# Row means from the rounded input, image row sums taken in the statistics pass, and a new order of TensorE's work in a two-layer convolution kernel

## What is computed

```python
# layer 0
n = 127.0
scale_input = max(abs(x_n)) / 128            # over the whole batch, x_n = group norm of x
x_q = round(clip(x_n / scale_input, -n, n))
acc = conv3x3(x_q, weight_int8)              # zero padding 1
x = x + acc * (scale_input * scale_weight) + bias
# layer 1
X = rfftn(group_norm(x), axes=(-2, -1))      # real and imaginary parts
Yr = conv3x3(Xr, wr) - conv3x3(Xi, wi) + b_real
Yi = conv3x3(Xr, wi) + conv3x3(Xi, wr) + b_imag
x = x + irfftn(Yr + i Yi)
```

## Time and profile before

| | us |
|---|---|
| median of 3 runs | 3694.32 (3689.42 to 3700.12) |
| the profiled execution, its own time | 3688.6 |
| its span in the profile | 3686.8 |
| TensorE busy (matmuls) | 2952.2, 80% of the span |
| VectorE busy | 3147.2, 85% |
| ScalarE busy | 1888.0, 51% |
| POOL busy | 1481.3, 40% |
| DMA | 730.98 MB, mean 198 GB/s |

### The profile page before, as it was taken

The page is one execution under the profiler, slowest core; times in us unless marked ns, Lnnn a source line. Parts: engine busy times, 40 slices in busy tenths (PEclk is TensorE's granted clock), DMA queues, the critical chain, the costliest instruction groups (busy, mean ns, idle before and its releaser), DMA issues.

```text
span 3686.8 us, 126585 instructions
## 1 busy us (share of the span) xinstructions
PE 2952.2 (80%) x45732; PEld 2630.6 (71%) x45732; DVE 3147.2 (85%) x5880; ACT 1888.0 (51%) x2799; POOL 1481.3 (40%) x1984
## 2 busy tenths in 40 slices
PE   0000004899999999999999999999999999999998
PEld 0000002688888888888888888888888888888888
DVE  8999995688888888888888888888888888888886
ACT  8999991344444444444444444444444444444443
POOL 4777100344444444434443333443443433344444
PEclk9999999999999999999999999999999999999999
DMA  8777760366666666666666666666666666666655
GB/s 312 239 239 239 239 216 13 100 205 197 201 199 203 202 200 200 204 197 200 201 202 195 197 194 193 202 197 197 204 199 196 204 194 192 201 193 206 199 181 180
DMA packets 630696, 730.98 MB, mean 198 GB/s; under 512 B 76752, under 2 KB 602160, under 8 KB 614736
## 3 DMA queue, kind: packets, MB, share of 16 engines
q1 hardware_dynamic: 482640, 588.71, 50.1%
q10 hardware_dynamic: 147456, 134.28, 12.7%
HBM read 262.58 MB, written 134.22 MB: 108 GB/s over the span
## 4 chain that ended last, share of the span: by engine, by line
PE 54%; SPq 13%; DMA 11%; issue 11%; DVE 7%; ACTq 1%; ACT 1%; POOL 1%; DVEq 0%; POOLq 0%
PE y_ps L986 14%; PE mean_b L1031 9%; PE x_ps L973 7%; PE conv_ps L1018 7%; SPq L464 7%; PE fin_ps L1005 6%; DMA halo<-quant 4%; DMA out<-img 4%; PE t_ps L964 4%; SPq L386 3%; PE conv_ps L1020 2%; DVE scaled L763 2%; DMA img<-in_x 2%; PE fin_ps L1000 2%; DVE scaled L764 1%
## 5 line engine op out<-in xcount | busy, mean ns | idle before, releaser
L734 POOL TENSOR_SCALAR eo<-img,norm 128x256 f32<-128x256 f32 x512 | 477.9, 933 | 1458.5 <-PE t_ps L964 1248.9
L986 PEld LDWEIGHTS y_ps<-mix_w,stack 128*128 128x128 f16 x24576 | 793.5, 99 | 119.6 <-DMA stack<-xn 6.0
L986 PE MATMUL y_ps<-mix_w,stack 128*128 128x64 f16 x24576 | 809.3, 194 | 4.5 <-DMA stack<-xn 4.4
L562 ACT ACTIVATE y_hi<-y_ps 128x512 f16<-128x512 f32 x512 | 305.6, 597 | 889.3 <-PE y_ps L986 889.3
L548 ACT ACTIVATE xt<-t_ps 128x512 f32<-128x512 f32 x512 | 305.7, 597 | 629.2 <-PE t_ps L964 506.6
L973 PE MATMUL x_ps<-dft,xt 128*128 128x128 f32 x4096 | 541.6, 275 | 0.0
L839 DVE SCALAR_TENSOR_TENSOR img<-conv_ps,cst,img 128x512 f32<-128x512 f32 x512 | 383.1, 748 | 169.3 <-PE conv_ps L1020 153.1
L1031 PE MATMUL mean_b<-row_mean,img 128*128 128x48 f32 x4096 | 512.8, 273 | 8.4 <-DVE img L839 8.4
L1031 PEld LDWEIGHTS mean_b<-row_mean,img 128*128 128x128 f32 x4096 | 504.1, 196 | 18.2 <-DVE img L839 17.5
L826 DVE SCALAR_TENSOR_TENSOR xn<-x_ps,norm,xn 128x512 f16<-128x512 f32 x512 | 383.7, 750 | 140.7 <-ACT xn L555 120.0
L973 PEld LDWEIGHTS x_ps<-dft,xt 128*128 128x128 f32 x4096 | 498.3, 192 | 0.0
(11 more groups left out here) (134 smaller groups left out, 5111.6 us busy)
## 6 DMA issues: line engine op xcount, KB each, us to landing
stack<-xn SPq DMA_DIRECT2D x2048, 132.0 KB, 2.7
img<-in_x SPq DMA_DIRECT2D x1024, 128.0 KB, 2.9
out<-img ACTq DMA_DIRECT2D x1024, 128.0 KB, 3.0
img<-in_x SPq DMA_DIRECT2D x120, 1024.0 KB, 4.9
halo<-quant SPq DMA_DIRECT2D x192, 193.3 KB, 3.3
halo<-quant SPq DMA_DIRECT2D x64, 169.1 KB, 3.2
row_mean<-table_row_mean SPq DMA_DIRECT2D x1, 768.0 KB, 15.4
spread<-table_spread SPq DMA_DIRECT2D x1, 512.0 KB, 14.6
```

The lines of the kernel that those rows point to most:

```text
L734: nc.gpsimd.tensor_scalar(even, rows[:, :, 0:F], norm[v][:, 2:3], None, ALU.add).then_inc(shift_s, 1)
L986: last = nc.tensor.matmul(y_ps[t % 2][:, g, b, :], stack[:, t % 2, g, first:first + F], mix_w[:, 2 * at + b, g, f, part, :], start=i == 0, ...
```

## The change

- The row means no longer come from the image after layer 0. They are put together from two parts. The weighted row sums of x itself are taken in the first phase (`image_means`): TensorE multiplies each image by the wave table as it passes, in fp32 (the table has 48 columns and is the weights, 256 image columns pass), ScalarE copies the 48 x 256 result out of PSUM, and SyncE writes it to DRAM (`keep`). In the second phase SyncE reads it back (`load_means`). The sums of the convolution follow from the same weighted sums of the rounded input: `row_means` multiplies the 16-bit rounded input by a 16-bit table of 128 columns, and `mean_rows` combines them with weights that POOL derives from the weights of layer 0.
- The waits of the first phase are extended: a quarter is reloaded only when TensorE is done with it too.
- ScalarE's scaling writes 16-bit integers (`whole`), which does the rounding; VectorE only limits them. quant and halo are fp16 instead of bf16.
- In TensorE's step, the convolution, its row means and the first group sum stand behind the mix; in VectorE's step `round_pair` stands ahead of `layer0_pair`.

```diff
-MEANS_OF = {14: (0, 1), 15: (2, 3), 0: (4, 5), **{t: (t + 5,) for t in range(1, 11)}}
-TABLES = ("dft", ..., "row_mean", ...)                   # 14 tables
+TABLES = ("sums_runs", "sums", "dft", ..., "coef_a", "rounded_w", ...)   # 17 tables
...
-        quant = sb("quant", [P, HB, HW], bf16)
-        halo = sb("halo", [96, HB, HW], bf16)
+        quant = sb("quant", [P, HB, HW], f16)
+        halo = sb("halo", [P, HB, HW], f16)
+        rounded_w = sb("rounded_w", [P, HB, P], f16)
+        rmx = sb("rmx", [48, 2, N])
...
+        whole = flat(scaled[:]).bitcast(mybir.dt.int16)[:, 0:2 * N].rearrange("p (a w) -> p a w", a=2)
...
         @block.sync
+            sp.dma_start(sums[1], table["sums_runs"]).then_inc(runs_s, 16)
             for u in range(2):
                 for q in range(QU):
                     load_runs(u + 2, u, q)
...
+            for g in range(R):
+                sp.dma_start(raw_a[C * g:C * g + C].rearrange("p o a b -> p o (a b)"), flat0).then_inc(weight_s, 16)
+            sp.dma_start(scale_o, scale_weight[None, :].to_broadcast([P, C])).then_inc(weight_s, 16)
...
+            def keep(n, k, u):
+                sp.wait_ge(sums_s, n + 3)
+                sp.dma_start(kept[k], rmx[:, u, :]).then_inc(kept_s[u], 16)
+
+            def load_means(k, u):
+                if not (isinstance(k, int) and k == 0):
+                    sp.wait_ge(meanc_s, k)
+                sp.dma_start(rmx[:, u, :], kept[k]).then_inc(rmx_s[u], 16)
...
+                        sp.wait_ge(p1_pe, (2 * i + u - 2) * QU + q + 1)
                         load_runs(2 * i + u + 2, u, q)
+                    keep(2 * i + u - 2, 2 * i + u, u)
...
                 for t in range(PAIRS):
+                    if t == 6 and conv:
+                        load_means(s + 1, 1 - u)
...
         @block.scalar
+                act.wait_ge(p1_pe, QU * (n + 1))
+                act.wait_ge(kept_s[u], 16 * (i + 1))
+                nc.scalar.activation(rmx[:, u, :], sums_ps[u], ACT.Copy).then_inc(sums_s, 1)
...
-                act.wait_ge(rounded_s, PAIRS * k + j)
-                nc.scalar.activation(scaled[:], img[u][:, 2 * j:2 * j + 2, :], ACT.Identity,
+                act.wait_ge(quant_s, PAIRS * k + j)
+                nc.scalar.activation(whole, img[u][:, 2 * j:2 * j + 2, :], ACT.Identity,
                                      bias=b0[:, bass.ds(k, 1)], scale=a0[:, bass.ds(k, 1)]).then_inc(scaled_s, 1)
...
+                    if conv and t == STATS_AT - 1:
+                        act.wait_ge(rq_s, PAIRS * (s + 3))
+                        nc.scalar.activation(rq[:], rq_ps, ACT.Identity, scale=q_scale).then_inc(rqe_s, 1)
...
         @block.vector
                 if not first:
-                    dve.wait_ge(conv_s, PAIRS * k + QP * (c + 1))
+                    dve.wait_ge(rq_s, PAIRS * k + QP * (c + 1))
                     dve.wait_ge(halo_s[c], 32 * k)
                 dve.wait_ge(scaled_s, PAIRS * k + j + 1)
                 rows = quant[:, 2 * j:2 * j + 2, 1:N + 1]
-                nc.vector.tensor_scalar(rows, scaled[:], MAGIC, MAGIC, ALU.add, ALU.subtract).then_inc(rounded_s, 1)
-                dve.wait_ge(rounded_s, PAIRS * k + j + 1)
-                nc.vector.tensor_scalar(rows, rows, CLIP, -CLIP, ALU.min, ALU.max).then_inc(quant_s, 1)
+                nc.vector.tensor_scalar(rows, whole, CLIP, -CLIP, ALU.min, ALU.max).then_inc(quant_s, 1)
...
+                    if conv if t < PAIRS - AHEAD else ahead:
+                        d, jq = quant_of(t)
+                        round_pair(s + d, jq, isinstance(i, int) and s + d == 0)
                     d, c = conv_of(t)
                     if conv if d == 1 else ahead:
                         layer0_pair(s + d, (u + d) % 2, c)
                     if conv and t == STATS_AT:
                         stats_var(s + 1)
-                    if conv if t < PAIRS - AHEAD else ahead:
-                        d, jq = quant_of(t)
-                        round_pair(s + d, jq, isinstance(i, int) and s + d == 0)
...
         @block.tensor
+            def image_means(i, u, tab):
+                n = 2 * i + u
+                for q in range(QU):
+                    pe.wait_ge(load_s[u][q], loaded(i))
+                    if q == 0:
+                        pe.wait_ge(sums_s, n + 1)
+                    for hb in range(QB * q, QB * q + QB):
+                        last = nc.tensor.matmul(sums_ps[u], tab[:, 48 * hb:48 * hb + 48], img[u][:, hb, :],
+                                                start=hb == 0, stop=hb == HB - 1)
+                    last.then_inc(p1_pe, 1)
...
-            def row_means(k, u, c):
-                pe.wait_ge(x1_s, done(k, c))
+            def row_means(k, c):
+                pe.wait_ge(quant_s, PAIRS * k + c + 1)
                 if c == 0:
-                    pe.wait_ge(meanc_s, k + 1)
-                    nc.tensor.matmul(mean_b[:, 0:96], ident[:], zeros[:], start=True, stop=False)
+                    pe.wait_ge(rqe_s, k + 1)
                 for hb in (2 * c, 2 * c + 1):
-                    for half in range(2):
-                        nc.tensor.matmul(mean_ps[half], img[u][:, hb, F * half:F * half + F], row_mean[:, hb, :],
-                                         start=False, stop=False)
+                    last = nc.tensor.matmul(rq_ps, rounded_w[:, hb, :], quant[:, hb, :], start=hb == 0, stop=hb == HB - 1)
+                last.then_inc(rq_s, 1)
-            def centre_rows(k, u):
+            def mean_rows(k, i, u):
+                pe.wait_ge(rmx_s[u], 16 * (i + 1))
+                pe.wait_ge(rqe_s, k + 2)
                 pe.wait_ge(zb_s, k + 1)
                 for half in range(2):
+                    for dw in range(3):
+                        nc.tensor.matmul(mean_ps[half], rq[:, F * half + dw:F * half + dw + F], conv_a[:, dw, :],
+                                         start=dw == 0, stop=False)
+                    nc.tensor.matmul(mean_ps[half], rmx[:, u, F * half:F * half + F], ident[0:48, 0:48], start=False, stop=False)
                     last = nc.tensor.matmul(mean_ps[half], norm[u][:, 2:3].to_broadcast([P, P]), channel[:],
...
                     if conv and t == IMAGE_AT:
-                        centre_rows(s + 1, 1 - u)
-                    d, means = means_of(t)
-                    if conv if d == 1 else ahead:
-                        for c in means:
-                            row_means(s + d, (u + d) % 2, c)
+                        mean_rows(s + 1, i + u, 1 - u)
+                    if conv and t == IMAGE_AT + 2:
+                        mix_rows(s + 1)
+                    if runs(mix, conv, t + 1):
+                        mix_pair(s, t + 1)
                     if conv and t == STATS_AT:
                         group_stat(s + 1, meane_s, 0, gmean_s)
                     d, c = conv_of(t)
                     if conv if d == 1 else ahead:
                         conv_pair(s + d, c)
-                    if conv and t == IMAGE_AT + 2:
-                        mix_rows(s + 1)
-                    if runs(mix, conv, t + 1):
-                        mix_pair(s, t + 1)
+                        for m in range(c) if d == 2 and c == 1 else ():
+                            row_means(s + d, m)
+                        if d == 1 or c:
+                            row_means(s + d, c)
```

More of the change, by code:

```diff
@@ L85, in shape_tables @@
             for r in range(R):
-                rm[:, r, b, j, :] = eye * wave[j, R * b + r] / N
-    tab["row_mean"] = rm.reshape(P, HB, 3 * C)
+                rm[0, :, r, b, j, :] = eye * wave[j, R * b + r] / N
+                rm[1, :, r, b, j, :] = eye * wave[j, HB * r + b] / N
+    tab["sums"], tab["sums_runs"] = rm.reshape(2, P, HB * 3 * C)
+    rw = np.zeros((P, HB, P), np.float16)
+    hi, lo = halves(RSCALE * N * rm[0].reshape(P, HB, 3 * C))
+    rw[:, :, 0:48], rw[:, :, 48:96] = hi, lo
+    for c in range(C):
+        rw[R * c, 0, 96 + c] = 1.0
+        rw[R * c + R - 1, HB - 1, 112 + c] = 1.0
+    tab["rounded_w"] = rw
+    ca = np.zeros((8, C, 3, 3))
+    for dh in range(3):
+        co, si = np.cos(th * (dh - 1)), np.sin(th * (dh - 1))
+        turn = np.array([[1, 0, 0], [0, co, si], [0, -si, co]])
+        for part in range(2):
+            ca[3 * part:3 * part + 3, :, :, dh] = (turn.T / (RSCALE * N))[:, None, :]
+    ca[6, :, :, 2] = -wave[:, N - 1] / N
+    ca[7, :, :, 0] = -wave[:, 0] / N
+    tab["coef_a"] = ca.reshape(P, 9)
     tab["channel"] = np.concatenate([np.repeat(eye, R, 0), np.zeros((P, 2 * C))], 1) / (2 * R)
@@ L147, in shape_tables @@
     tab["coef_i"] = ci
[L149 removed]
+    half = ("inv", "spread", "first_row", "rounded_w")
     return {n: np.ascontiguousarray(v, dtype=np.float16 if n in half else np.float32) for n, v in tab.items()}
@@ L169, in build @@
     table = {k: nc.inline_tensor(v, name=f"table_{k}").ap() for k, v in shape_tables().items()}
+    kept = nc.dram_tensor("kept", (samples, 48, N), fp32, kind="Internal").ap()
     ctx = ExitStack()
@@ L242, in build @@
```

(20 more changed lines are left out.)

68 lines of the change are left out of this document (46 added, 22 removed).

## The result

The changed kernel takes **3660.0 us** (median of 6 runs, 3651.4 to 3672.5) against 3693.3 us (3686.2 to 3701.8) for the kernel before, measured in turn on the same chip: ratio 0.991, 95% interval 0.9885 to 0.9935. It is faster, but by 33 us and not by 206; the time is outside the predicted range. The profiled execution after has a span of 3649.5 us, against 3686.8: 37.3 us less.

The account below looks back on a forecast made before the run. The prediction took TensorE to bound the kernel, with SyncE's DMA-issuing queue close below and the bound afterwards. 3688.6 - 194 (steady stage) + 12 (start) - 25 (first image) + 2 (end) = 3483, at the median 3488 us; range 3335 to 3612.

Parts of the forecast that it names:

- SyncE's waits in the sum for the period: Steady stage: SyncE's 86.1 to 89.7 us plus at most some 2 of waits gives 88 a period, 194 us gained in all.
- TensorE's stall at step 10: Steady stage: the variance matmul waits for VectorE's late layer 0, about 2 us a period, for which TensorE has room.
- TensorE's work: Steady stage: row means go and smaller matmuls come, so TensorE's busy time falls from 90.7 to 82.4 us a period.
- VectorE: Steady stage: rounding goes, limit on integers takes 0.30 us; busy time falls from 80.0 to 72.8 us a period, hidden.
- Start: Before the third image: added tables and weight DMAs on SyncE, 10.5 us, and 1.8 MB more to move; +12 us.
- First image: First image's convolution: row means of 1.94 us leave the loop 16 times, less halo waits and longer mean_rows; -25 us.
- End: End of the kernel, from 3593 us on, without convolution: +2 us for mean_rows.
- The two engines hinder each other: Rival, steady stage: SyncE flat out at 89.7 us plus 2 of waits, period 92, median 3612 us; chance 0.18.
- No gain in the steady stage: Rival: SyncE's issues lengthen with the rate and eat everything, 3678 to 3690 us; chance 0.04.
- TensorE stays the bound: Rival, steady stage: SyncE's long issues shrink as stores spread out, period 83.5 us, median 3348 us; chance 0.20.
- SyncE's long issues: Single SyncE issues up to 2203 ns (median 603), taken as waits for ScalarE's stores through a shared descriptor generator; period then nearer 86.1.
- The half-rate first phase: Rival, first phase: TensorE at half rate needs 28.5 us an image instead of 17.6, median 3838 us; chance 0.08.

Follow-up runs that it names:

- a_stats_first: The changed kernel with VectorE's group variance ahead of `layer0_pair` at step 10; 3581.3 us, ratio 0.970 to the kernel before.
- a_half_loads: The changed kernel with one of the two image loads of each step issued by ScalarE instead of SyncE; 3513.6 us, ratio 0.950 to the kernel before.
- b_round: The kernel before with only the rounding done by ScalarE's 16-bit integer write, VectorE keeping just the limit; 3696.5 us, ratio 0.9996.
- b_no_means: The kernel before without the fp32 row means except for the first pair (30 of 32 row blocks left out); 3642.7 us, ratio 0.983.
- a_order_old: The changed kernel with the old order of TensorE (convolution ahead of mix) and VectorE (`layer0_pair` ahead of `round_pair`); 3700.9 us, ratio 1.001 to the kernel before.
- b_order_new: The kernel before with TensorE's row means, convolution and first group sum moved behind the mix; 3826.3 us, ratio 1.035.
- b_order_nomeans: The kernel before with row means, convolution and first group sum behind the mix, and 30 of 32 row blocks left out of the means; 3640.0 us, ratio 0.981.
- a_loads_act: The changed kernel with both image loads of a step issued by ScalarE, behind its stores, instead of SyncE; 3533.2 us, ratio 0.955 to the kernel before.

## Why the prediction was wrong

**The step that failed** is SyncE's waits in the sum for the period: "I take 88 us a period, between 86.1 and 89.7, with no waiting on top of the upper and some 2 us on top of the lower". It measured 93.75. SyncE's work was right (85.2 us; predicted 86.1, with one DMA more than before). The waits were wrong, 8.5 us in place of 2. I had argued that the loads "shed most of that" because the stores come 1.7 us earlier in the step. They shed 1.5 us a period, and waits for the mix gave 1.1 of it back. The mistake in kind was to split 94.3 us into 85.4 of work and 8.9 of slack. This queue, which works in order and needs 85 to 87 us of 94, did not absorb a stall of two microseconds that comes every period. In the changed kernel too it ran eight steps in 43.5 us, 5.44 us each as in the earlier trace rows, right behind a pause of 2.7 us:

```profile
1509.77 2.56 SPq L519 DMA_DIRECT2D stack<-xn  x4
1515.00 1.39 SPq L417 DMA_DIRECT2D img<-in_x  x2
...
1558.53 1.39 SPq L417 DMA_DIRECT2D img<-in_x  x2
```

a_stats_first shows it from the side of the wait, a_half_loads from the side of the work. What the remaining 5.6 us of waits for stores come from (the latency of the landing, or the place of the store in ScalarE's step) no run tells apart.

**TensorE's stall at step 10** was foreseen ("about 2 us a period on TensorE, which now has room for it"), 2.08 us measured. That TensorE had room for it was the second error: the next restacking waits for the mix behind it, so it went through SyncE's queue to everything. And nothing in my sum had the fall of the clock in the steady stage, where all figures were taken at full rate. **TensorE's work** was right: predicted 82.4 us, measured 85.0, of which 98.7 / 2000 x 93.75 / 2 = 2.3 are half rate, leaving 82.7.

**VectorE** 72.1 us (predicted 72.8). The limit on integers takes 0.32 us on average (0.31 in the kernel before), ScalarE's integer write 0.80, as its fp32 write did; b_round confirms that in the total it's worth nothing. **Start** +10.2 (predicted +12): VectorE's second idle time is 14.5 us, was 6.27, and its first 7.90, was 5.87. The two tables and nine DMAs of the prediction come to 10.0 us, not 10.5; the table ahead of all loads, which had next to nothing in that sum, cost 2.0. **First image** -32.9 (predicted -25), b_no_means gives -17 for leaving out the row means. a_order_old, whose first mark is at 659.7, gives -11 for the new order of both engines. TensorE's half of that order had no part in it in the kernel before (first mark 671.4 in b_order_new, 654.7 in b_order_nomeans, as in the old order), so VectorE's half, the rounding ahead of `layer0_pair`, is the likely source; no run has it alone. Another 2 us are the rounding itself (b_round, 669.8). **End** +1.0 (predicted +2). The prediction's total is rounded down by 1 us: its terms give 3483.6, and 3489 at the median.

**The rivals.** "The two engines hinder each other" was nearest in mechanism, SyncE's queue as the bound with waits on top, and missed its sizes: 89.7 us of work and 2 of waits, where 85.2 and 8.5 were measured. "No gain in the steady stage" is what came, but not by its reason: the issues did not lengthen (four restacking DMAs 2.86 us on average, 2.85 before; two loads 1.49, 1.52 before), and its total, 3678 to 3690, is 18 us and more too high. "TensorE stays the bound" is refuted by the chain and by a_loads_act. SyncE's long issues, which the prediction tied to ScalarE's stores, are not all explained by these: of the 275 issues over 0.7 us between 1000 and 3000 us, 113 overlap no issue of ScalarE in the trace. The half-rate first phase is refuted: TensorE is busy for 85.33 of 100 us at a granted clock of 0.95, then 87.10 at 0.91; it runs at half rate in stretches, catches up, and VectorE's 100.00 of 100 hides it all. The clock did play a part, in the stage where I had not looked for it. One reading of the prediction needs a word: the row that it quotes for 600 to 671 us shows a granted clock of 1.00, and yet it speaks of 1.2 GHz. The trace of the kernel before has no record of the clock ahead of 685.8 us, where it has the first one, at full rate, and the view shows 1.00 for times without a record. So the half rate there rests on the pace of the matmuls alone (1.28 us for three, 0.65 later).

The Trainium skill (TensorE: Matmul & The Clock Gate, Part 1) states that sustained activity is what releases the clock. The first phase agrees: gaps between quarters, a clock of 0.91 to 0.95, no lasting loss. In the steady stage a stall came again each period, and behind 18 of the 22 the full rate was lost again, for 68 us in all.

## What to carry to other kernels

Before a gain is credited to an engine, add up work and waits of every in-order queue, and ask of each wait whether the queue could make it up in the same loop; here, with work of 91% of the period, the one wait that a run took away came back in full (2.4 us of period for a stall of 2.08). A stall of TensorE can cost more than its length, through the clock behind it and through the queue that waits for what comes next, so look for a small operation on another engine that could simply stand earlier. When a DMA-issuing queue is the bound, move issues to another engine, but only behind work that is not in the loop; the same move gained 3.5% in the changed kernel and lost 1.6% in the kernel before, in whose order of work it stood in TensorE's loop.

## What the runs showed of the hardware

- The time in which SyncE issues a DMA hardly depended on what it moves: 2.89 us for four of 33 KB, 2.86 us for four of 132 KB. Single issues took twice as long and more (1.26 us at 1536.30 us after, against a median of 0.60; up to 2.2 in the earlier trace rows); what lengthens them no run tells, and ScalarE's issues alone do not account for it (113 of 275 long ones overlap none).
- The granted clock fell to half rate behind stalls of TensorE of some 2 us, with the engine busy for 96% of the stage: 150 us in 2000 in b_order_new, with a stall of 2.08 us per period, against 27 in the kernel before; at 19 of its 20 stalls the clock fell. Leaving out work had the same effect (198 us in b_no_means, where TensorE waits more): 12.5 us fewer of work, 8.7 us fewer of busy time.
- A write of ScalarE to 16-bit integers, and a VectorE operation on them, took the time of their fp32 and bf16 forms: 0.80 us (0.81 before) and 0.32 us (0.31 before) for 512 elements in each of 128 partitions.
